# Interleaving the next head's QKV projection with the attention of the current head

## The reference

```
x = x + layernorm(attention(layernorm(x), w_qkv, w_out))
x = x + layernorm(ffn(layernorm(x), weight, lora_A, lora_B, router_w))

attention: qkv = x @ w_qkv ; q = q / sqrt(128)
           scores = q k^T, causal mask, softmax ; out = attn v ; out @ w_out
ffn:       base = x @ weight^T ; probs = softmax(x @ router_w^T), top 2 of 8, renormalised
           Ax = x lora_A^T ; expert_out = sum of the two experts' (Ax * w) lora_B * 2
           base + expert_out
```

## Time and profile before

| | us |
|---|---|
| median of 3 runs | 2242.58 (2232.15 to 2244.6) |
| the profiled execution | 2245.44 |
| its span, slowest core | 2243.7 |
| spans of the eight cores | 2215.5 to 2243.7 |
| PE busy | 1732.9 (77%) |
| DVE busy | 692.6 (31%) |
| ACT busy | 692.0 (31%) |
| POOL busy | 42.1 (2%) |

### The profile page before, as it was taken

One profiled execution on the slowest core, in us unless ns is written; L12 is line 12 of the kernel. 1 busy time (PEld: TensorE's weight loads), 2 busy tenths in 40 slices (PEclk: granted clock), 3 DMA queues, 4 the chain that ended last, 5 costly groups with the idle time before them and its releaser, 6 DMA issues.

```text
span 2243.7 us, 25832 instructions; the slowest of 8 cores (2215.5 to 2243.7 us)
## 1 busy us (share of the span) xinstructions
PE 1732.9 (77%) x9552; PEld 902.6 (40%) x9552; DVE 692.6 (31%) x1697; ACT 692.0 (31%) x1009; POOL 42.1 (2%) x59
## 2 busy tenths in 40 slices
PE   1258988988978978978978879870999906888886
PEld 1124444444444444444544444440444403444442
DVE  4542222222222222222222222230233312454443
ACT  4533032032132132132131131230233322656564
POOL 0000000000000000000000000000000000000000
PEclk9998978978978978978878878875999957898997
DMA  8312012022022022022022020009122284010101
GB/s 184 117 57 29 5 25 29 2 28 29 1 29 29 1 29 28 1 29 29 1 29 29 1 29 1 1 1 158 48 76 76 78 136 68 38 57 38 57 39 56
DMA packets 48633, 95.07 MB, mean 42 GB/s; under 512 B 5248, under 2 KB 38144, under 8 KB 42368
## 3 DMA queue, kind: packets, MB, share of 16 engines
q0 software_dynamic: 46064, 76.58, 18.8%
q1 hardware_dynamic: 2448, 16.85, 2.2%
HBM read 119.67 MB, written 16.78 MB: 61 GB/s over the span
## 4 chain that ended last, share of the span: by engine, by line
PE 59%; ACT 15%; DVE 12%; issue 7%; another core or an unknown queue 5%; DMA 1%; DVEq 0%; ACTq 0%; POOL 0%; SPq 0%; POOLq 0%
PE P_qkv L291 30%; PE P_qkv L460 10%; ACT expT L399 8%; PE P_e L541 5%; PE P_o L541 5%; DVE sst L151 5%; ACT expT L425 2%; PE P_qkv L416 2%; DVE ost L797 2%; PE P_sc L388 2%; ACT x2s L791 1%; PE P_b L704 1%; ACT xln L633 1%; PE P_b L760 1%
## 5 line engine op out<-in xcount | busy, mean ns | idle before, releaser
L291 PE MATMUL P_qkv<-A,wbf 128*128 128x512 bf16 x3072 | 666.9, 379 | 14.9 <-DVE A L371 14.2
L291 PEld LDWEIGHTS P_qkv<-A,wbf 128*128 128x128 bf16 x3072 | 299.6, 98 | 377.1 <-issue 19.0
L425 ACT ACTIVATE expT<-P_sc,cbuf 128x512 bf16<-128x512 f32 (+1 forms) x128 | 74.9, 585 | 817.4 <-PE P_sc L416 816.7
L460 PE MATMUL P_qkv<-Vaug,expT 128*128 128x129 bf16 x2176 | 256.8, 302 | 25.1 <-DVE srcp L471 13.7
L460 PEld LDWEIGHTS P_qkv<-Vaug,expT 128*128 128x128 bf16 x2176 | 222.7, 141 | 46.9 <-issue 46.8
L704 PE MATMUL P_b<-A,x2T 128*128 128x512 bf16 x1024 | 231.5, 388 | 0.4 <-DVE sff L769 0.4
L399 ACT ACTIVATE expT<-P_sc,cbuf 128x1024 bf16<-128x1024 f32 x96 | 107.3, 1118 | 210.0 <-PE P_sc L388 210.0
L541 PE MATMUL P_e<-wo_bf,A 128*128 128x512 bf16 x512 | 114.1, 384 | 57.9 <-DMA wo_bf<-w_out 57.9
L704 PEld LDWEIGHTS P_b<-A,x2T 128*128 128x128 bf16 x1024 | 101.7, 100 | 123.3 <-issue 10.6
L440 DVE TENSOR_TENSOR expT<-expT,cbuf 128x256 bf16<-128x256 bf16 x128 | 37.4, 292 | 334.8 <-ACT expT L425 334.8
L541 PE MATMUL P_o<-wo_bf,A 128*128 128x512 bf16 x512 | 111.8, 379 | 0.0
(11 more groups left out here) (86 smaller groups left out, 1434.1 us busy)
## 6 DMA issues: line engine op xcount, KB each, us to landing
wbf<-wqkv POOLq DMA_DIRECT2D x16, 1536.0 KB, 16.1
expT<-x SPq DMA_DIRECT2D x16, 1024.0 KB, 6.1
xio<-x POOLq DMA_DIRECT2D x16, 1024.0 KB, 6.2
out<-ost POOLq DMA_DIRECT2D x16, 1024.0 KB, 4.2
wo_bf<-w_out POOLq DMA_DIRECT2D x2, 4096.0 KB, 43.4
A<-weightT POOLq DMA_DIRECT2D x2, 4096.0 KB, 42.9
sat<-at POOLq DMA_DIRECT2D x1, 512.0 KB, 60.5
sbf<-bflat POOLq DMA_DIRECT2D x1, 512.0 KB, 62.1
```

Source lines behind the costliest of these rows:

```text
L291: _q=col0, _p=wpar: e.matmul(P_qkv[:, _q:_q + 512], wbf[:, 6144 * _p + 384 * _c + 128 * _m: 6144 * _p + 384 * _c + 128 * _m + 128], A1[:, ...
L425: _u=sub, _o=128 * s: e.activation(expT[:, 512 * _i + _o: 512 * _i + 512], _s[:, 512 * _u + _o:512 * _u + 512], AF.Exp, bias=EBIAS, scale= ...
L460: _q=qt: e.matmul(P_qkv[:, _a:_a + 129], expT[:, 512 * _i + 128 * _u: 512 * _i + 128 * _u + 128], Vaug[:, 129 * _i:129 * _i + 129], start= ...
```

## The change

1. Qbf, Kbf and VTs get two buffers, one for even and one for odd heads.
2. The projection is cut into 12 units of 16 matmuls with their DVE move (`make_qkv_units`). They use banks 0 and 1 in turn. Head 0's units run ahead of the loop. Within head h the units of head h+1 are emitted by `pump(n)`: one behind each score pair, one behind the second and one behind the fourth diagonal tile, one at the end of each query block, and what is left at the end of the head.
3. All scores go to the one slot P_sc (banks 4 and 5). The AV matmuls go to banks 2 and 3.
4. The weight DMA of head h+1 is recorded at the start of head h's query blocks.
5. In phases 1 and 4 the normalised tile is written by one ACT instruction of 2048 columns in place of two of 1024, and all transposes wait for it.

```diff
-            for h in range(H):
...
-                        bp = [2 * half, 2 * half + 1]
-                        gww = B.gw(bp)
+                def mk(m, half, tb, first):
+                    col0 = 1024 * half + 512 * tb
+                    def unit():
+                        bank = gidx[0] % 2
+                        gidx[0] += 1
+                        gw = B.gw([bank])
+                        for ch in range(NCH):
...
+                            B.emit("tensor", lambda e, _c=ch, _m=m, _q=col0,
+                                   _p=wpar, _b=bank: e.matmul(
+                                       P_qkv[:, 512 * _b:512 * _b + 512],
...
+                        B.sg([bank], c["dve"], ev)
...
+            wsem0, wrdy0 = plan_wdma(0)
+            for u in make_qkv_units(0, wsem0, wrdy0):
+                u()
+            for h in range(H):
+                hb = h % 2
...
+                if h + 1 < H:
+                    wsemN, wrdyN = plan_wdma(h + 1)
+                    units = make_qkv_units(h + 1, wsemN, wrdyN)
+                else:
+                    units = []
+                ui = [0]
+                def pump(n):
+                    for _ in range(n):
+                        if ui[0] < len(units):
+                            units[ui[0]]()
+                            ui[0] += 1
...
-                        slot, bnks = pair_slots[sc_seq % 2]
-                        sc_seq += 1
+                        gwp = B.gw([4, 5])
...
-                        B.sg(list(bnks), c["act"], ev)
+                        B.sg([4, 5], c["act"], ev)
+                        pump(1)
                     for s in range(4):
...
+                        if s % 2 == 1:
+                            pump(1)
...
-                        avsl = (qt % 2) * 512
-                        bank = qt % 2
+                        avsl = 1024 + 512 * (qt % 2)
+                        bank = 2 + qt % 2
...
+                    pump(1)
+                pump(12)
```

The edit in phase 1 (the one in phase 4 is of the same kind):

```diff
-                xlvh = []
-                for hf in range(2):
-                    xlvh.append(B.emit(
-                        "scalar", lambda e, _p=bpar, _r=rstd, _m=negmr,
-                        _x=xio, _h=hf: e.activation(
...
+                xlv = B.emit("scalar", lambda e, _p=bpar, _r=rstd, _m=negmr,
+                             _x=xio: e.activation(
+                                 xln[:, 2048 * _p:2048 * _p + 2048],
+                                 _x, AF.Identity, bias=_m, scale=_r),
```

More of the change, by code:

```diff
@@ L321, in build_program @@
-                    if m == 1:
-                        vt_block = [0, 0, 0, 0]
-                B.sg([("wbf", wpar)], c["pe"], c["pe"].v)
-                vt_dve = c["dve"].v
+                            units.append(mk(m, half, tb, first))
+                            first = False
+                return units
+            wsem0, wrdy0 = plan_wdma(0)
[3 more added lines that the diff above has]
+                hb = h % 2
                 for grp in range(2):
@@ L383, in build_program @@
                     for i0 in range(0, 4 * qb, 2):
[L384 to L385 removed]
+                        gwp = B.gw([4, 5])
                         for d in range(2):
                             B.emit("tensor", lambda e, _i=i0 + d, _qb=qb,
[L388 to L391 removed]
+                                   _d=d, _hb=hb: e.matmul(
+                                       P_sc[:, 512 * _d:512 * _d + 512],
+                                       Kbf[:, 2048 * _hb + 128 * _i:
+                                           2048 * _hb + 128 * _i + 128],
+                                       Qbf[:, 2048 * _hb + 512 * _qb:
+                                           2048 * _hb + 512 * _qb + 512],
                                        start=True, stop=True),
[L393 to L394 removed]
+                                   waits=(gwp + [(c["dve"], vaug_dve)])
                                    if d == 0 else (),
@@ L449, in build_program @@
                         mask_done[4 * qb + 2 * w + 1] = pv
-                    for u in range(4):
-                        qt = 4 * qb + u
-                        avsl = (qt % 2) * 512
-                        bank = qt % 2
+                    for u2 in range(4):
+                        qt = 4 * qb + u2
+                        avsl = 1024 + 512 * (qt % 2)
+                        bank = 2 + qt % 2
                         wts = B.gw([bank]) + [(c["act"], exp_done[qt]),
```

186 lines of the change are left out of this document (87 added, 99 removed).

## The result

| | kernel before | changed kernel |
|---|---|---|
| median (lowest to highest) of 23 runs each | 2244.65 (2231.4 to 2398.15) | 2217.39 (2210.2 to 2449.65) |
| ratio of the runs, 95% interval | | 0.9894 (0.9871 to 0.9918) |
| profiled execution | 2245.44 | 2213.83 |
| spans of the eight cores | 2215.5 to 2243.7 | 2205.6 to 2212.2 |

The change makes the kernel 1.1% faster: 24 us by the ratio, 27 us by the medians, 31.5 us between the spans of the two profiled executions. The forecast was 2219 us. The highest times, here and in the experiments, are of executions in which the cores of one die ran slower, whichever the kernel; the medians hold them and the ratios leave them out.

The account below looks back on a forecast made before the run. PE was taken as the bound, with holes waiting for exps and a falling clock. Fifteen heads gain 39.0 us, the last loses 13.9, phases 1 and 4 cancel: 2220 profiled, 2219 median; 8 in 10 range 2196 to 2264.

Parts of the forecast that it names:

- Dense units at full clock: Projection units in the attention's holes: twelve of 3.46 us, 82.1 us per head if the clock never falls into one.
- falls: Half clock entering units after the seam or the AV parts of blocks 0 and 1: one in three heads, 0.6 us.
- case (a): Rival: one fall of the clock in each head, 83.8 us per head, 2237 us; chance 0.18.
- Case (b): Rival: units start at half clock in two places of each head, 85.5 us per head, 2262 us; chance 0.15.
- The mask behind the move: Blocks 0 and 1: PE waits 1.4 us for DVE's mask, queued behind the unit's move, two waits per head.
- One slot in block 3: Block 3 without units: each pair waits for the exp of the pair before, 13.1 us against 6.0.
- case (d): Rival: the clock holds in block 3, 78.8 us per head, 2161 us; chance 0.04.
- The last head: The head without units and with only one score slot: 13.9 us lost.
- Phase 1 and phase 4: One ACT instruction per tile: 5 to 7 us lost in the first, 5 to 7 gained in the other, cancelling.
- Free switches and a free weight DMA: In the heads, pairs and units run back to back, and the later weights' DMA costs nothing.
- Case (c): Rival: each of some 16 switches in a head costs PE 0.14 us, 84.9 us per head, 2253 us; chance 0.07.
- signs of being wrong: Unit starts 0.43 us apart over whole units in every head, or PE idle ahead of L415 or L443 in blocks 0 to 2.

Follow-up runs that it names:

- e10: e9 with the projection cut into 24 half units of 8 matmuls, one for each hole, masks ahead of the unit: 1854.72 us, ratio 0.8293.
- e3: The changed kernel with the two DVE masks of a query block emitted ahead of the second unit's move: 2183.01 us, ratio 0.9746.
- e8: The changed kernel with four filler matmuls that nothing reads behind each of block 3's pairs: 2183.61 us, ratio 0.9761.
- e4: The changed kernel with two score slots once a head's units are used up: 2111.74 us, ratio 0.9437.
- e1: The kernel before with only the one ACT instruction per tile in phases 1 and 4, attention untouched: 2243.14 us, ratio 1.0012.
- e5: The changed kernel with the twelve units behind the twelve score pairs only, still one score slot: 2079.48 us, ratio 0.9309.
- e9: e5 with two score slots in the last head alone and phase 1 in halves: 2054.65 us, ratio 0.9185.

## Why the prediction was right

**Dense units at full clock: right.** Matmuls of 512 columns start 216 ns apart, not 214 as I wrote ahead of the prediction; the 3.46 us of a unit is unchanged by it. Terms against the head of core 2, less 3.46 us per unit (2 in block 0's stretch, 5 each in those of blocks 1 and 2):

| us | seam | block 0 | block 1 | block 2 | block 3 | head, no fall | falls | head |
|---|---|---|---|---|---|---|---|---|
| predicted | 3.3 | 4.0 | 5.3 | 6.9 | 21.1 | 82.1 | 0.6 | 82.7 |
| measured | 3.2 | 4.1 | 5.3 | 7.0 | 20.8 | 81.9 | 0.75 | 82.65 |

The falls are the mean (1239.8 / 15 = 82.65) less the clean head; core 2's heads lie between 81.6 and 84.2. They strike in two of the three places that the prediction named, never behind the seam. By the granted clock of the eight cores a fall follows the thin AV part of block 0 in 17 of the 120 heads and that of block 1 in 26: one in 2.8 heads, where I had guessed one in three. That was a guess between no fall and one, so its closeness is luck; on core 2 it was seven of fifteen. Its basis was also read too widely: on core 7 of before only the first five heads took 81.7 us, and from the seventh on 85.3 like the others. The fall behind block 1 in the first head of core 2, then busy time behind block 0 in the second head, and the first unit behind it (15 matmuls listed, 5.09 us):

```profile
233.20:236.60 3.40, 3.18 (x15) 1.63 (x14) 1.13 (x5) 0.00 (x0) 0.00 (x0) 0.50 0.00 0
...
290.00:294.00 4.00, 1.83 (x17) 0.95 (x16) 2.50 (x11) 0.00 (x0) 0.00 (x0) 1.00 0.00 0
294.00:298.00 4.00, 3.95 (x15) 1.57 (x14) 0.97 (x5) 0.00 (x0) 0.00 (x0) 0.58 0.02 4
```

The second head took 84.2 us: case (a), one fall. Case (b), which would have made the kernel slower, needed two in every head on the mean. e10 shows the other end of the same mechanism: with half units in those places no fall is left in heads 1 to 14.

**The mask behind the move: right.** Two waits per head, in blocks 0 and 1, and 0.18 in block 2. The bracket says 1.15 us and not 1.4 because it counts from the modelled end of the last matmul. From the end of its streaming (787.45 + 16 x 0.216 = 790.91) to the first AV matmul at 792.22 it is 1.31. e3 took the wait away and gained 2.3 us per head, about what two of them are worth.

**One slot in block 3: right, with one period mis-sized.** I had three of the six periods at 1.95 us and three at 2.42. The trace has four at 1.95 and two at 2.37: 12.5 against 13.1; the AV part took 5.9 against 5.6. Against two slots the loss is 5.9 us per head on the mean. Heads without any half clock compare at 78.9 us with one slot (e8) and 73.9 with two (e4), so 5.0 us are the wait itself. The clock costs 3.0 us in a clean head of the changed kernel and on the mean 2.9 in e4 (76.8 less 73.9), so it weighs on both sides.

**The clock in block 3 (case (d)): it fell, as the row of before had it.** The granted clock was 0.71, then 0.57 in the head shown, though no wait of PE in block 3 was longer than 1.36 us. The section "A second HAM failure mode: psum-queue depth-cycling" of the Trainium skill's page "TensorE: Matmul & The Clock Gate" describes this better than the section that the prediction weighed: short pauses between groups of matmuls, repeated, make the clock swing. The trace agrees: the pauses here are 1.35 us each, and e8, which left the pairs 1.95 us apart and shortened the pauses to 0.49, kept 1.00 in these scores.

**The last head: sign right, the size 3 us too high.** 54.8 against 44.0 is +10.8, where 13.9 was predicted. I had put all pairs of blocks 1 and 2 at 2.42 us. The two of block 1 are at 2.39 on the mean, nearly as priced. But the clock rose again within the dense AV parts of blocks 1 and 2, and the pairs behind them began at full clock: two of four at 1.95 in block 2 (8.6 us where 9.7 was priced) and three of six in block 3 (12.9 where 13.6 was). That is 1.8 of the 3 us; the rest I have not itemised. The timeline, core 2, block 2 of head 15:

```profile
1456.95 0.59 PE L415 MATMUL P_sc<-Qbf,Kbf 128*128 128x512 bf16 x2 [1.35 <-ACT expT L427]
1458.90 1.01 PE L415 MATMUL P_sc<-Qbf,Kbf 128*128 128x512 bf16 x2 [1.35 <-ACT expT L427]
1461.27 1.01 PE L415 MATMUL P_sc<-Qbf,Kbf 128*128 128x512 bf16 x2 [1.35 <-ACT expT L427]
1463.63 0.91 PE L443 MATMUL P_sc<-Qbf,Kbf 128*128 128x512 bf16 x2 [1.35 <-ACT expT L427]
```

**Phase 1 and phase 4: phase 1 larger than priced, phase 4 as priced for a tile.** Phase 1, core 2, the changed order of the earlier trace rows:

```profile
68.19 2.09 ACT L221 ACTIVATE xln<-expT,sst 128x2048 bf16<-128x2048 f32 x1 [0.47 <-DVE sst L178]
...
70.54 1.86 PE L234 MATMUL P_qkv<-cbuf,xln 128*128 128x128 bf16 x16 [7.13 <-ACT xln L221]
71.23 1.70 DVE L243 COPY A<-P_qkv 128x512 bf16<-128x512 bf16 x4 [3.18 <-PE P_qkv L234]
```

PE starts 2.35 us after ACT, not 2.04 to 2.2; before it was 1.49. The instruction took 2.09 us, above the 1.89 to 2.06 that I had taken from its neighbours, and its end comes to PE 0.26 us later, not 0.15. A tile takes 9.0 us (DVE's sums at 63.85 and 72.85) where 8.8 was predicted, 0.6 more than before: +7.7 and +8.3 on cores 1 and 2 against 5 to 7. Phase 4, the row answering to the earlier trace rows:

```profile
1973.51 0.22 PE L781 MATMUL P_x<-cbuf,su 128*128 128x128 bf16 x1 [1.83 <-ACT su L768]
```

PE's wait for su fell from 2.27 to 1.83 us and the tile, by the stores of out over fourteen tiles, from 22.49 to 22.09 us: 15 x 0.4 = 6.0 us, within the 5 to 7. Against core 1 of before the whole stage is 7.5 to 9.7 us shorter, but on the mean of the eight cores 4.4, so more than the price isn't shown. e1 has both edits alone, and no difference in the time.

**Free switches and a free weight DMA: right.** Case (c) wanted 0.14 us per switch between pair and unit; e5's 3.89 us per pair and unit leaves nothing for it, and the changed kernel has the same 3.89 (pairs at 797.82 and 801.71 us, core 2). Over the fifteen heads the view of waits lists no wait of PE for a DMA. One of the signs of being wrong did appear by its words: PE waits ahead of L443 in blocks 0 and 2 (1.31, 0.77 and 0.20 us, core 2). These are the wait for Vaug ahead of the first score and the bare diagonal of block 2, which the sum had priced; the sign was too wide.

**The sum.** Between the slowest cores of the profiled executions: -40.1 (predicted -39.0), +10.8 (+13.9), +8.3 (+5 to 7), -7.5 (-5 to -7), and -2.9 in the stages that are the same: 31.5 us less, where 25 was predicted. The heads and the last head both came out better than priced, by 1.1 and 3.1 us, phase 1 worse by some 2. By the profiled executions the forecast was 6 us off (2220 against 2213.83). That the medians agree within 2 us (2219 and 2217.39) is luck: I had put the median 3 us under the profiled execution, and it came out 3.6 above it. The times of the rivals (2237, 2262, 2253, 2161) are of the profiled execution and would be 3 us lower on the forecast's scale.

## What to carry to other kernels

Dense independent work put between dependent ones pays by how it is dealt out: the same 192 matmuls gained 1.1% in twelve pieces that left block 3 bare and 6.9% behind the twelve pairs (e5); with two slots in the last head and phase 1 in halves beside it, 8.2% behind the pairs (e9) and 17.1% in 24 pieces with one for each hole (e10). So count the holes first (here twelve pairs, four diagonals, the seam, the AV parts), cut the work until there is a piece for each, and give none to a hole that is covered already. A stretch left without such work should keep its second buffer: with 3.46 us of cover PE never waited for the one slot (e5), and without cover a pair took 1.95 us where two slots give one per 1.00 us. And wherever work of two streams meets in an in-order queue, record first what the bottleneck engine waits for next: here two small masks ahead of one 0.69 us move were worth more than the change itself (e3).
